# A transformer block with cross attention and two MoEs in one kernel: gate and up of the last MoE as three f32r products, six row buffers, and the first attention operands split one stage earlier

## The reference

```
x = x + attention(layernorm(x), context)   # 16 heads, 4 kv heads of 128, RMS norm, rope, causal over x, context keys in front
x = x + moe_two_of_eight(layernorm(x))     # 8 experts of 128 in bf16, top 2, and a shared one
x = x + memory_attention(layernorm(x), context, mask)
x = x + moe(layernorm(x)):                 # the stage called "slots" below
    route = sigmoid(x @ router_w);  e = argmax(route);  p = max(route)
    out = p * (silu(x @ gate_w[e]) * (x @ up_w[e])) @ down_w[e]     # 8 experts, 256 -> 512 -> 256
```

## Time and profile before

| | us |
|---|---|
| median of 3 runs (lowest, highest) | 3123.14 (3123.08, 3124.46) |
| the profiled execution | 3123.67 |
| its span, first to last instruction | 3121.9 |
| PE, DVE, ACT, POOL busy | 2891.9, 2181.1, 2030.9, 1612.4 |
| mean granted TensorE clock | 0.971 of full speed |

### The profile page before, as it was taken

One profiled execution on the slowest core, in us unless ns is written; L12 is line 12 of the kernel. 1 busy time (PEld: TensorE's weight loads), 2 busy tenths in 40 slices (PEclk: granted clock), 3 DMA queues, 4 the chain that ended last, 5 costly groups with the idle time before them and its releaser, 6 DMA issues. The chain is left out here.

```text
span 3121.9 us, 61580 instructions
## 1 busy us (share of the span) xinstructions
PE 2891.9 (93%) x18731; PEld 2450.3 (78%) x18731; DVE 2181.1 (70%) x4611; ACT 2030.9 (65%) x5169; POOL 1612.4 (52%) x2087
## 2 busy tenths in 40 slices
PE   5887999899999999999999999999999977699698
PEld 4665888678888888888888888888888854388654
DVE  7995444577777777777777777777777767766443
ACT  5664666677777777777777777777777647666111
POOL 6993333455555555555555555555555344465122
PEclk9998999999999999999999999999999979899699
DMA  4335666610110110110110110110110010353511
GB/s 134 116 118 175 202 202 203 201 62 33 52 46 33 53 46 33 52 46 33 53 46 33 52 46 33 53 46 33 53 46 33 1 46 1 99 158 113 177 33 28
DMA packets 244462, 236.02 MB, mean 76 GB/s; under 512 B 11654, under 2 KB 224527, under 8 KB 244208
## 3 DMA queue, kind: packets, MB, share of 16 engines
q1 hardware_dynamic: 225552, 212.01, 20.7%
q10 hardware_dynamic: 16448, 15.73, 1.7%
q0 software_dynamic: 2208, 5.12, 0.6%
HBM read 148.93 MB, written 84.80 MB: 75 GB/s over the span
## 5 line engine op out<-in xcount | busy, mean ns | idle before, releaser
L911 ACT ACTIVATE pt_hi<-ps_t 128x512 fp32r<-128x512 f32 (+2 forms) x1024 | 570.4, 557 | 412.9 <-PE ps_t L1156 409.7
L983 DVE TENSOR_REDUCE piece_max<-ps_s 128x1 f32<-128x512 f32 (+2 forms) x1024 | 631.7, 622 | 257.1 <-PE ps_s L1143 229.5
L1009 DVE TENSOR_TENSOR pt_lo<-ps_t,pt_hi 128x512 fp32r<-128x512 f32 (+2 forms) x1024 | 656.4, 641 | 200.5 <-ACT pt_hi L911 184.3
L1083 POOL TENSOR_SCALAR prob<-prob,inv_sum 128x512 f32<-128x512 f32 (+2 forms) x1024 | 639.4, 645 | 268.5 <-DVE inv_sum L999 268.5
L899 ACT ACTIVATE prob<-ps_s,neg_max 128x512 f32<-128x512 f32 (+2 forms) x1024 | 649.2, 634 | 87.6 <-DVE neg_max L990 70.9
L1176 PE MATMUL ps_o<-pt_hi,v_hi 128*128 128x256 f32 (+1 forms) x1856 | 595.4, 321 | 0.0
L1156 PE MATMUL ps_t<-ident,prob 128*128 128x128 f32 (+1 forms) x3712 | 571.9, 272 | 1.4 <-DVE pt_lo L1009 1.3
L1178 PE MATMUL ps_o<-pt_hi,v_lo 128*128 128x256 f32 (+1 forms) x1856 | 523.2, 282 | 0.0
L1177 PE MATMUL ps_o<-pt_lo,v_hi 128*128 128x256 f32 (+1 forms) x1856 | 522.3, 281 | 0.0
L1156 PEld LDWEIGHTS ps_t<-ident,prob 128*128 128x128 f32 (+1 forms) x3712 | 456.2, 140 | 60.7 <-issue 1.6
L1138 PE MATMUL ps_s<-k_hi,q_hi 128*128 128x512 f32 (+2 forms) x1024 | 403.8, 394 | 35.0 <-ACT prob L899 20.0
(11 more groups left out here) (262 smaller groups left out, 5621.4 us busy)
## 6 DMA issues: line engine op xcount, KB each, us to landing
v_scratch<-v_out SPq DMA_DIRECT2D x120, 256.0 KB, 2.5
raw_k<-k_scratch SPq DMA_DIRECT2D x32, 960.0 KB, 5.3
raw_v<-v_scratch SPq DMA_DIRECT2D x32, 960.0 KB, 4.7
k_scratch<-k_out SPq DMA_DIRECT2D x104, 256.0 KB, 2.6
q_scratch<-out_t SPq DMA_DIRECT2D x64, 256.0 KB, 2.6
raw_q<-q_scratch SPq DMA_DIRECT2D x32, 512.0 KB, 3.3
c_raw<-in_ctx_t ACTq DMA_DIRECT2D x52, 256.0 KB, 2.8
raw_t<-in_ctx_t SPq DMA_DIRECT2D x24, 512.0 KB, 4.1
```

What stands on the lines that cost most here:

```text
L911: nc.scalar.activation(pt_hi[keys, k % RING, cols], ps_t[keys, k % 2, cols], ACT.Copy).then_inc(hi_done, 1)
L983: nc.vector.tensor_reduce(piece_max[:, n % 2, p:p + 1], ps_s[:, p, lo - p * PC:hi - p * PC], AX.X, ALU.max).then_inc(max_ready, 1)
L1009: nc.vector.tensor_tensor(pt_lo[keys, k % RING, cols], ps_t[keys, k % 2, cols], pt_hi[keys, k % RING, cols].bitcast(F32), ALU.subtract).th ...
L1083: nc.gpsimd.tensor_scalar(prob[:, n % PB, lo:hi], prob[:, n % PB, lo:hi], inv_sum[:, n % PB:n % PB + 1], 1.0, ALU.mult, ALU.mult).then_inc ...
```

## The change

1. The constants' block goes; the four DVE operations stand behind the first body of the context stage.
2. The parts of q, k and v of group 0 are made in the last three bodies (twelve tiles) of context_projections: 18 pieces (8 wo, 6 q/k, 4 v), two and one by turns per tile, high parts on ACT behind copy_k, low parts on DVE one piece later. The start of attention loses them.
3. route_to_slots: xn is written over x_sb, for which DVE waits until x_rows is stored. Gate and up each have their own landing semaphore. Behind the sigmoid ACT makes 16 high parts of 128x1024 (one per expert for gate, then up); POOL makes the low parts of the first 12, in place of the raw weights, and DVE those of the last 4, behind expert_of and before fact.
4. moe_slots: gate and up are three f32r products (12 matmuls of 128x512 where 4 in f32 stood, which are 8 records); copy_x becomes high_x on ACT and low_x on DVE, and turn_x and hidden wait for low_x; RING is 6.

The diff, cut:

```diff
@@ context_projections
+        def operands_at(i, t):
+            if not isinstance(i, int) or i < NB - END_BODIES:
+                return []
+            at = (i - NB + END_BODIES) * TB + t
+            first_n = at + (at + 1) // 2
+            return range(first_n, first_n + 2 - at % 2)
...
                         copy_k(i, t)
-                        if not loads:
-                            high_wo(t + (TB if last else 0))
+                        for n in operands_at(i, t):
+                            high_operand(n)
...
                             sum_squares(i, t + LEAD)
-                        if last:
-                            low_wo(t)
+                        for n in operands_at(i, t):
+                            if n:
+                                low_operand(n - 1)
@@ attention
-                for x in range(KQ_PIECES):
-                    split_kq(0, 0, x)
-                for x in range(V_PIECES):
-                    split_v(0, 0, x)
@@ route_to_slots
-        xn = sb("xn6", [P, NT, D])
+        xn = x_sb
+        LATE = E1 // 2
+        def low_w(engine, vector, n):
+            m, e = divmod(n, E1)
+            engine.wait_ge(w_hi_done, n + 1)
+            vector.tensor_tensor(weights[m][:, e, :, :].bitcast(F32R), weights[m][:, e, :, :], weights_hi[m][:, e, :, :].bitcast(F32), ALU.subtract).then_inc(w_split, 1)
...
                 nc.vector.tensor_copy(expert_of[:, :], passed_min[:, :]).then_inc(table_ready, 1)
+                for n in range(2 * E1 - LATE, 2 * E1):
+                    low_w(dve, nc.vector, n)
                 dve.wait_ge(held, 1)
...
                 nc.scalar.activation(score[:, :, :], ps_l[:, :].rearrange("p (t e) -> p t e", t=NT), ACT.Sigmoid).then_inc(scored, 1)
+                high_w(0)
+                high_w(1)
...
                     norm_rstd(nc, pool, mean_var, rstd, half, norm, part)
+                for n in range(2 * E1 - LATE):
+                    low_w(pool, nc.gpsimd, n)
@@ moe_slots
-    RING = 4
+    RING = 6
...
                     for ps, w, done in ((ps_g, gate_w, gate_done), (ps_u, up_w, up_done)):
                         for c in range(DC):
-                            last = nc.tensor.matmul(ps[:, :], xt[:, s % 2, c, :], w[:, bass.ds(e, 1), c, :].rearrange("p a n -> p (a n)"),
-                                                    start=c == 0, stop=c == DC - 1)
+                            nc.tensor.matmul(ps[:, :], x_hi, w_hi, start=c == 0, stop=False)
+                            nc.tensor.matmul(ps[:, :], x_hi, w_lo, start=False, stop=False)
+                            last = nc.tensor.matmul(ps[:, :], x_lo, w_hi, start=False, stop=c == DC - 1)
...
+                def low_x(s):
+                    dve.wait_ge(xt_hi_done, s + 1)
+                    if s >= 2:
+                        dve.wait_ge(up_done, s - 1)
+                    nc.vector.tensor_tensor(xt_lo[:, s % 2, :, :], ps_x[:, 0:D].rearrange("p (c n) -> p c n", c=DC),
+                                            xt_hi[:, s % 2, :, :].bitcast(F32), ALU.subtract).then_inc(xt_lo_done, 1)
...
                     nc.vector.tensor_copy(ht[:, :, :], ps_h[:, :].rearrange("p (c n) -> p c n", c=HC1)).then_inc(ht_copied, 1)
+                    if s + 2 < ESLOTS:
+                        low_x(s + 2)
                     if s >= 1:
                         finish(s - 1)
```

More of the change, by code:

```diff
@@ L482, in context_projections @@
     WO_HEADS = NH // WO_PIECES
-    _, _, _, _, _, wo_hi, wo_lo = operands
+    _, _, _, kq_loaded, v_loaded, wo_hi, wo_lo, first, (kq_hi, kq_lo, vv_hi, vv_lo) = operands
+    q0, k0, v0 = first[0:2], first[2:4], first[4:6]
     with ExitStack() as ctx:
@@ L790, in attention_operands, with kq_piece, v_piece @@
     sb, _, sem = scope(ctx, nc)
+    first = [sb(f"{name}_{part}0", shape, F32R) for name, shape in OPERANDS for part in ("hi", "lo")]
     return (sb("raw_q", [P, GRP, L]), sb("raw_k", [P, NK]), sb("raw_v", [P, KB * HD]), sem("kq_loaded"), sem("v_loaded"),
-            sb("wo_hi", [P, NH, D], F32R), sb("wo_lo", [P, NH, D], F32R))
+            sb("wo_hi", [P, NH, D], F32R), sb("wo_lo", [P, NH, D], F32R), first,
+            (sem("kq_hi_split"), sem("kq_lo_split"), sem("v_hi_split"), sem("v_lo_split")))
+def kq_piece(operands, q, k, x):
+    if x < 2:
+        h = slice(2 * x, 2 * x + 2)
+        return operands[0][:, h, :], q[0][:, h, :], q[1][:, h, :]
+    k_cols = slice((x - 2) * KPIECE, (x - 1) * KPIECE)
+    return operands[1][:, k_cols], k[0][:, k_cols], k[1][:, k_cols]
+def v_piece(operands, v, x):
+    cols = slice(x * PC, min((x + 1) * PC, KB * HD))
+    return operands[2][:, cols], v[0][:, cols], v[1][:, cols]
 def load_kq(sp, it, q_dram, k_dram, operands):
-    raw_q, raw_k, _, kq_loaded, _, _, _ = operands
+    raw_q, raw_k, _, kq_loaded = operands[:4]
     sp.dma_start(raw_q[:, :, :], q_dram[bass.ds(it, 1)].rearrange("a p h q -> p (a h) q")).then_inc(kq_loaded, 16)
@@ L801, in load_v @@
 def load_v(sp, it, v_dram, operands):
-    _, _, raw_v, _, v_loaded, _, _ = operands
+    _, _, raw_v, _, v_loaded = operands[:5]
     sp.dma_start(raw_v[:, :], v_dram[bass.ds(it, 1)].rearrange("a p k n -> p (a k n)")).then_inc(v_loaded, 16)
 def attention(nc, q_dram, k_dram, v_dram, x_sb, ident, ident_bf, mask_bf, operands):
-    raw_q, raw_k, raw_v, kq_loaded, v_loaded, wo_hi, wo_lo = operands
+    _, _, _, kq_loaded, v_loaded, wo_hi, wo_lo, first, (kq_hi, kq_lo, vv_hi, vv_lo) = operands
     with ExitStack() as ctx:
         sb, psum, sem = scope(ctx, nc)
[L810 to L815, removed]
+        second = [sb(f"{name}_{part}1", shape, F32R) for name, shape in OPERANDS for part in ("hi", "lo")]
+        q_hi, q_lo, k_hi, k_lo, v_hi, v_lo = zip(first, second)
         prob = sb("prob", [P, PB, NK])
@@ L1137, in scores @@
                     qs = slice(qt * P, qt * P + P)
[L1138 to L1139 removed]
+                    nc.tensor.matmul(out, q_hi[gi][:, h, qs], k_hi[gi][:, lo:hi], start=True, stop=False)
+                    nc.tensor.matmul(out, q_hi[gi][:, h, qs], k_lo[gi][:, lo:hi], start=False, stop=False)
                     if p == 0:
@@ L2342, in _, with high_w @@
                     nc.scalar.activation(xt[:, g % 2, :], ps_t[:, g % 2, :], ACT.Copy).then_inc(xt_copied, 1)
+                def high_w(m):
+                    act.wait_ge(w_loaded[m], 16)
+                    for e in range(E1):
+                        nc.scalar.activation(weights_hi[m][:, e, :, :], weights[m][:, e, :, :], ACT.Copy).then_inc(w_hi_done, 1)
                 act.wait_ge(logits, NT // 2)
                 nc.scalar.activation(score[:, :, :], ps_l[:, :].rearrange("p (t e) -> p t e", t=NT), ACT.Sigmoid).then_inc(scored, 1)
+                high_w(0)
+                high_w(1)
             @block.gpsimd
@@ L2497, in _ @@
                 normalise(1)
+                low_x(0)
+                low_x(1)
                 for s in range(ESLOTS):
```

134 lines of the change are left out of this document (74 added, 60 removed).

## The result

| | us |
|---|---|
| changed kernel, median of 7 runs (lowest, highest) | 3136.24 (3134.81, 3138.25) |
| kernel before, median of 7 runs on the same chips | 3124.11 (3122.91, 3127.60) |
| ratio, 95% interval | 1.0039 (1.0027 to 1.0050) |
| profiled execution, and its span | 3134.81, 3133.0 |

What follows compares the result with a forecast made beforehand. PE was taken as fullest, nine tenths or more busy in context projections and attention; the change touches places where it is not full. 3123.67 - 1.0 - 6.8 - 2.7 + 20 = 3133.2 us, range 3109 to 3141.

Steps and rivals of the forecast that it cites:

- Constants' block: Before the context stage: its four DVE operations move into slack, so the next load starts earlier, -1.0 us.
- Joint: Between context stage and attention: first score 7.4 us earlier, less 0.6 for a later stage end, together -6.8 us.
- Rival 4: At the joint: no gain, because the last context tiles run late by as much; 3140 us, chance 0.05.
- Slots: Last MoE: period from 6.47 to 6.37 us over twenty slots, -2.0; with start and tail, -2.7 us.
- Routing: Routing: DVE operations with two SBUF inputs wait for POOL's weight subtractions, delaying the block's end by 20 us.
- What PE lost is 5.1 us on ht and 10.4 on xn: Last MoE's slots in the kernel before: PE's own losses in waits, against 77.4 us of DVE's xn waiting for rows.
- nearly all of it becomes a stall: Last MoE's slots: of 15 us of PE work saved (23 times 0.66), nearly all turns into PE stall.
- Rival 1: Routing: DVE's chain hardly waits for POOL, so the block ends with POOL, +11.3 us, 3124.5 us; chance 0.17.
- Rival 2: Last MoE's slots run at PE's pace, period 5.2 us, 3110 us, faster by 13 us; chance 0.18.
- Rival 3: Last MoE's slots: PE's queue is late from address operations, 0.4 us per slot, +8, 3141 us; chance 0.10.

Runs made afterwards that it cites:

- e12: The changed kernel with DVE's low parts in the context stage taken one per tile, the last seven behind the last normalisation: 3135.64 us in one run.
- e8: The changed kernel with DVE taking each low part in the context stage two pieces behind ACT's high part, not one: 3137.95 us in one run.
- e3: The changed kernel with low_x(s+1) behind hid(s) in DVE's queue, in place of low_x(s+2) ahead of finish, silu and hid: 3113.35 us, ratio 0.9958.
- e1: The changed kernel with POOL's twelve weight subtractions moved to DVE, which makes all sixteen, twelve of them behind the routing: 3126.64 us, ratio 1.0005.
- e5: The kernel before with six row buffers in place of four in the last MoE, gate and up still in f32: 3112.57 us, ratio 0.9958.
- e9: The changed kernel with all sixteen weight subtractions on DVE, eight in its waits and eight behind the routing, plus the edits of e3 and e12: 3093.78 us.
- e7: The changed kernel with the edits of e1, e3 and e8 together: 3101.84 us, ratio 0.9927.
- e11: The changed kernel with the weight subtractions in pieces twice as long, six on POOL and two on DVE: 3138.66 us in one run.

## Why the prediction was right

The forecast was 3133.0 (range 3109 to 3141, slower 0.58); the median is 3136.24 and the profiled execution 3134.81 against a sum of 3133.2. Term by term, against the profiles:

- **Constants' block**, -1.0: right, the load is 0.96 earlier. That is one pair of profiles: it stands between 259.7 and 262.5 in the twelve with the changed front, at 261.6 and 262.1 in the two others.
- **Joint**, -6.8: it gave about -3.6 behind the earlier load. The mis-sized term is "delays the last normalisation and store by some 0.6 us"; it was 3.4 to 3.8. I had followed ACT's catch-up and costed DVE's low parts at nothing, though they stand in the queue of the same chain as POOL's root (sq_sum, rms, normed). How much of it is theirs stays open: e12 shows 0.5 for their standing in pairs, e8 shows that the wait for wo_hi is not it, and what is left is read from traces and not tested. Rival 4 had the kind right and the size too large.
- **Slots**, -2.7: measured -4.0. The period was to be 6.37 and is 6.31 (126.1 us for the twenty periods that the prediction put at 127.4), PE's stall 1.08 and is 0.92, and it stands where the prediction put it, before ps_h behind low_x, finish, silu and hid. e3 shows the cause: that queue order, not the work.
- **Routing**, +20: measured +20.4. e1 shows that POOL's twelve subtractions cause it all. The mechanism was narrower than the truth. The prediction let only operations with two SBUF inputs wait and had the lane masks waiting for POOL; in fact own, best_f, onehot_bf, share_int, slots, first_row and slot_part, with one input, wait as well, so POOL's twelve pieces are used up before the lane masks, which run free. Both ways nearly every POOL piece holds one DVE operation, so the sum hardly moved. That the two lists, twelve expected and eleven measured, come within 0.4 us of each other is luck in part. The Trainium skill (SBUF — State Buffer, Who interferes with whom) says that copy, cast and tensor_scalar may take the port pair in a 2-port mode and that tensor_reduce never does. The trace agrees: 2.39 us for the cast best_f, 0.22 for the reduction end. The sum by that rule was put 1.3 us higher, 21.3; it is 20.4.

The total is nearer than its terms: against the spans the joint gave 3.2 us less than forecast, the slots 1.3 more, the routing cost 0.4 more, and 0.7 came from the stretch between, which says nothing. Two small products of the working are off and touch no term: 16 copies at 1.06 from 2932.9 end at 2949.9, and four times two times 0.6 is 4.8 (the trace has 15.3 us for the copies and 4.6 for the four subtractions). Two of the signs that were named did not show: the first score stands at 617.69 and not at 614.5, and the lane masks of DVE are not long.

**The step that the sum hid.** "What PE lost is 5.1 us on ht and 10.4 on xn" and "nearly all of it becomes a stall" left the slots' two parts in one term. e5 and e3 take them apart. Six buffers alone take 12.8 us off, since the waits of the wait table are only the ends of a loop of 6.5 us (behind PE's first start they come to 9.0). The f32r products with low_x ahead of silu then bring 8.7 us back (138.9 in place of 130.2 between the first and last turn_x), and with low_x behind hid they save 13.9 (116.3). The -2.7 was near as a sum of a gain and a loss that I had not priced apart.

**The rivals.** Rival 1 (the chain hardly waits for POOL, 3124.5) is refuted by e1 and by the 2.4 us operations. Rival 2 (slots at PE's pace, 3110) did not happen, but its price was right once the order was changed: 5.19 us a slot, and 3113 in e3. Rival 3 (PE's queue late): its waits marked "issue" before gate are two, 0.7 us in all, so no.

Not tried: ACT's catch-up in the context stage by itself; starting the weight loads earlier than the routing.

## What to carry to other kernels

Work given to an idle POOL is not free while DVE runs a chain of small operations: here the chain lost 20 to 22 us for 27 to 28 us of POOL's work, whatever the piece size. The same work on DVE itself, twice as fast there (1.15 us a piece in e1, 2.32 on POOL), brought the first product 10 us forward (e1), and half of it laid in DVE's waits 19 us (e9). In a software pipeline, write down the loop through each buffer ring and each engine's queue order before pricing a faster matmul: in the slots the same products lost 8.7 us or gained 13.9 by the place of one operation of 0.4 us. A wait row names where a loop ends, not what it costs; take the period against the undisturbed period instead.

## What was not expected of the hardware

- POOL is held up by DVE too. Its first three indirect gathers take 1.23, 0.95 and 0.95 us to issue alone, and 1.54, 1.69 and 1.92 us beside DVE's weight subtractions in e1 (1.55, 1.69 and 1.84 in e7; 1.54, 1.69 and 1.91 in e9).
- Short copies are held as well as long ones: 128x16 in f32, 0.16 us in e1, takes 2.07 beside POOL and 2.85 in e11.
- The same end of a stage can run at either of TensorE's two clock levels. In the changed kernel PE waits 2.52 and then 2.30 us before the transposes of the context stage's last two tiles; its granted clock is 0.62 from 608 to 611 and 0.50, the lower level (1.2 GHz), from 611 to 613, and the last four transposes take 1.11 us. In the kernel before only the last of them stood behind such a wait (2.40 us), the clock was 0.83 from 608 to 611, and they took 0.70. One would put the 0.4 us down to the change. But e5, with the front of the kernel before and the same waits (0.74 and 2.40 us), has a granted clock of 0.74 from 608 to 611 and 0.50 from 611 to 613, and its last four transposes, at 610.60, take 1.11 us too. So the 0.4 us is not shown to belong to the change.
